# Half of a feed-forward chunk moved into the last attention step of a one-core transformer layer

## The reference

```
qkv = x @ w_qkv.T + b_qkv                      # x: (2, 1024, 512)
attn = softmax(q @ k.T / sqrt(32) + causal)    # per head, in float32
x = layernorm(x + (attn @ v) @ w_out.T + b_out)
hidden = relu((x @ sign(up_weight).T) * up_scale)
out = (hidden @ sign(down_weight).T) * down_scale * output_scale
return layernorm(x + out)
```

## Time and profile before

| | us |
|---|---|
| median of 3 runs | 776.65 (772.4 to 778.32) |
| the profiled execution | 774.34 |
| its span, first to last instruction | 772.6 |
| PE busy | 722.7 (94%) |
| DVE busy | 450.5 (58%) |
| POOL busy | 354.4 (46%) |
| ACT busy | 317.2 (41%) |

### The profile page before, as it was taken

How to read it: one execution, slowest core, us unless ns; L and a number is a source line. 1 busy time by engine, 2 the same in 40 slices (tenths; PEclk the granted TensorE clock), 3 DMA queues, 4 the chain that set the end, 5 groups by cost and what they waited for, 6 DMA issues and landing times.

```text
span 772.6 us, 11683 instructions
## 1 busy us (share of the span) xinstructions
PE 722.7 (94%) x4032; PEld 505.2 (65%) x4032; DVE 450.5 (58%) x1086; ACT 317.2 (41%) x631; POOL 354.4 (46%) x487
## 2 busy tenths in 40 slices
PE   6899999999999999999979889999999999999993
PEld 4788665655656556565544544788778787878882
DVE  4176495785967859678567751633294339334515
ACT  5211365654655546555546565432232222122210
POOL 4461467394673946739423502632353235223333
PEclk9999999999999999999999999999999999999998
DMA  6976464435544355452677331313012001000101
GB/s 231 296 208 177 110 174 124 136 105 163 150 132 132 108 157 148 115 133 88 174 206 261 109 123 58 120 32 119 14 41 95 28 1 41 15 1 12 44 1 54
DMA packets 44619, 85.71 MB, mean 111 GB/s; under 512 B 4880, under 2 KB 13584, under 8 KB 44432
## 3 DMA queue, kind: packets, MB, share of 16 engines
q1 hardware_dynamic: 35536, 79.72, 34.2%
q10 hardware_dynamic: 9024, 5.24, 2.4%
HBM read 55.33 MB, written 29.36 MB: 110 GB/s over the span
## 4 chain that ended last, share of the span: by engine, by line
PE 71%; DVE 19%; issue 3%; DMA 3%; POOL 2%; ACT 2%; SPq 0%; ACTq 0%; POOLq 0%
PE ps_heads L1045 9%; PE ps_proj L1087 7%; DVE heads_sb L835 7%; PE ps_proj L947 7%; PE ps_score L1104 6%; PE ps_unit L1063 6%; PE ps_unit L1087 5%; PE ps_sum L1039 5%; DVE maxes L813 5%; PE ps_unit L983 4%; PE ps_heads L1104 3%; PE ps_unit L1015 3%; PE ps_sum L1104 3%; PE ps_score L1015 2%; PE ps_score L983 2%
## 5 line engine op out<-in xcount | busy, mean ns | idle before, releaser
L655 POOL TENSOR_TENSOR hid_low<-hid_raw,hid_high 128x512 fp32r<-128x512 f32 x64 | 85.1, 1330 | 175.0 <-DVE hid_high L886 171.9
L711 ACT ACTIVATE probs<-ps_unit 128x512 f32<-128x512 f32 (+3 forms) x216 | 101.9, 490 | 88.4 <-PE ps_unit L1015 85.0
L619 POOL TENSOR_SCALAR_AFFINE_SELECT probs<-probs 128x128 f32<-128x128 f32 x256 | 73.1, 298 | 113.0 <-ACT probs L711 108.9
L711 ACT ACTIVATE probs<-ps_score 128x512 f32<-128x512 f32 (+3 forms) x155 | 75.2, 498 | 77.0 <-PE ps_score L1015 75.6
L886 DVE CAST hid_high<-hid_raw 128x512 fp32r<-128x512 f32 x64 | 27.1, 424 | 125.4 <-ACT hid_raw L766 125.2
L809 DVE CUSTOM_DVE_ANT_0 ps_unit<-ps_unit,causal 128x512 f32<-128x512 f32 (+3 forms) x162 | 80.1, 511 | 32.5 <-PE ps_unit L983 31.5
L1045 PE MATMUL ps_heads<-probs,v_rows 128*32 128x512 f32 (+3 forms) x768 | 80.3, 502 | 11.8 <-DVE heads_sb L837 11.8
L983 PE MATMUL ps_unit<-stack 96*128 96x512 f32 (+3 forms) x246 | 83.8, 354 | 5.7 <-DVE maxes L809 2.5
L1015 PE MATMUL ps_unit<-stack 98*128 98x512 f32 (+2 forms) x216 | 78.4, 366 | 4.1 <-DVE maxes L809 4.0
L613 POOL TENSOR_TENSOR parts<-qk_full,parts 128x512 fp32r<-128x512 f32 x32 | 41.3, 1289 | 64.7 <-ACT parts L690 64.4
L835 DVE RECIPROCAL heads_sb<-ps_sum 128x128 f32<-128x128 f32 x64 | 60.8, 950 | 9.2 <-PE ps_sum L1039 9.2
(11 more groups left out here) (195 smaller groups left out, 1478.0 us busy)
## 6 DMA issues: line engine op xcount, KB each, us to landing
stack<-qk_parts SPq DMA_DIRECT2D x96, 256.0 KB, 4.6
qk_parts<-parts SPq DMA_DIRECT2D x32, 512.0 KB, 2.9
v_all<-h_even ACTq DMA_DIRECT2D x16, 256.0 KB, 3.8
v_rows<-v_all SPq DMA_DIRECT2D x8, 512.0 KB, 4.3
heads_t<-heads_sb SPq DMA_DIRECT2D x16, 256.0 KB, 3.4
raw<-up_w SPq DMA_DIRECT2D x8, 512.0 KB, 3.9
x_tile<-x_rows SPq DMA_DIRECT2D x16, 256.0 KB, 5.5
raw<-down_w SPq DMA_DIRECT2D x8, 512.0 KB, 3.4
```

The costliest lines, as they stand in the source:

```text
L655: nc.gpsimd.tensor_tensor(hid[1][:, (HM * s + n) % 3, :], hid_raw[:, n % 2, :], hid[0][:, (HM * s + n) % 3, :].bitcast(FP32), ALU.subtract ...
L711: nc.scalar.activation(probs[:, (NP * s + n) % RING, 0:width], bank(what, s, n)[:, off:off + width], ACT.Exp, scale=SCALE).then_inc(s_exp, 1)
```

## The change

The first chunk's feed-forward is cut into two rounds of two tiles. Round 0 (tiles 0 and 1, matmuls of 256 columns in `up`, half as many in `down`) is placed in step 7 from slot 16 on, one pair each 1.95 slots, with hidden buffers of its own; it adds into two of the `ps_unit` banks. Round 1 (tiles 2 and 3) has the place of the old first chunk and 16 slots. With it:

- Scores of step 7 from piece 17 on rotate over two banks, and over three before that.
- In step 6, norm of the first half goes from slot 18.4 to 19.25, pv groups 4 to 6 go to 28, 30 and 32.2, and the last projection (k = 3) goes from slot 11.9 to 19.4; its keep goes from 19.9 to 29.4 and its stack from 22.2 to 31.9.
- Fetch 0 goes from slot 30 to 27.2, fetch_x 0 from 31 to 28.5. Jobs 0 and 1 go from 17.2 to 28, their signs from 23 and 25.5 to 31 and 33.5. All other jobs follow each 3.6 slots, with up and down weights in turn, and end in step 7.
- The output projection of tiles 0 and 1 goes into the end of step 6, that of tiles 2 and 3 early into step 7; layer norm and turns come some 13 slots earlier, over three banks.
- The last norm of step 7 goes to slots 55 to 58.6, inside round 1. The next chunk's split, projection and turns are packed over the 16 slots of round 1.

```
-ALONE = [[11.2, 13.5, 15.7, 18.3, 24, 28, 31.5, 36, 39.5, 43, 46.5, 50.3],
-ALONE_NORM = [[18.4, 18.41, 18.42, 18.43, 50.4, 50.41, 50.42, 50.43],
-              [17.6, 17.61, 17.62, 17.63, 48.7, 48.71, 48.72, 48.73]]
+ALONE_NORM = [[19.25, 19.26, 19.27, 19.28, 50.4, 50.41, 50.42, 50.43],
+              [17.6, 17.61, 17.62, 17.63, 55, 56.2, 57.4, 58.6]]
...
-LAST_BLOCK = [(1, 2, 4.2, 0.48, 9.9, 12.5, 14.9), (1, 3, 11.9, 0.45, 17.1, 19.9, 22.2)]
+LAST_BLOCK = [(1, 2, 4.2, 0.48, 9.9, 12.5, 14.9), (1, 3, 19.4, 0.62, 26.7, 29.4, 31.9)]
...
+ROUNDS = [(0, (0, 1)), (0, (2, 3))] + [(i, tuple(range(TT))) for i in range(1, CH)]
+TILES = [0, 2, 4, 8, 12, 16]
+FILL_FROM = 17
+
+JOBS = [("out", 0), ("out", 1), ("up", 0), ("up", 1), ("down", 0), ("up", 2), ("down", 1), ("up", 3), ("down", 2), ("up", 4),
+        ("down", 3), ("up", 5), ("down", 4), ("up", 6), ("down", 5), ("up", 7), ("down", 6), ("down", 7)]
...
-    signs = [late + 23, late + 25.5] + [late + 29 + 4.6 * k for k in range(4)] + [late + 50.2 + 4.5 * k for k in range(4)]
-    signs += [late + 88, late + 92] + [FIRST_UP + 1, FIRST_UP + 3] + [FIRST_UP + 7 + 2 * k for k in range(4)]
+    last = NP * (STEPS - 1)
+    signs = [late + 31, late + 33.5] + [late + 37 + 3.6 * k for k in range(16)]
-        put(late + 17.2 if k < 2 else signs[k - 2] + (3 if k < 4 else 0.5), "job", 0, k)
+        put(late + 28 if k < 2 else signs[k - 2] + 0.5, "job", 0, k)
...
-    last = NP * (STEPS - 1)
-    put(late + 30, "fetch", 0)
-    put(late + 31, "fetch_x", 0)
+    put(late + 27.2, "fetch", 0)
+    put(late + 28.5, "fetch_x", 0)
     put(last + 12, "fetch", 1)
+    for i in range(TT):
+        put(late + 36 + 1.7 * i, "split", 0, i)
+        put(late + 40 + 1.3 * i, "bias", 0, i)
         for m in range(12):
-            put(last + 0.5 + 5.2 * i + 0.42 * m, "attn", 0, 12 * i + m)
-        put(last + 5.8 + 5.2 * i, "y", 0, i)
-        put(last + 23 + i, "norm1", 0, i)
-        put(last + 26 + 2.5 * i, "turn", 0, i)
-    put(last + 22.5, "std1", 0)
+            put((late + 44.5, late + 47.1, last + 2.5, last + 5.5)[i] + 0.22 * m, "attn", 0, 12 * i + m)
+        put((late + 47, last + 2.2, last + 7.7, last + 8.2)[i], "y", 0, i)
+        put(last + 9.4 + 0.1 * i, "norm1", 0, i)
+        put((last + 12.9, last + 13.4, last + 15.2, last + 15.7)[i], "turn", 0, i)
+    put(last + 9.3, "std1", 0)
+    for r, (i, tiles) in enumerate(ROUNDS):
+        t = FIRST_UP + 16 * (r - 1)
         for m in range(HM):
-            put(t + m, "up", i, m)
-            if i < CH - 1 or m < HM - 2:
-                put(t + m + 2.5, "down", i, m)
-        if i == CH - 1:
-            for q in range(TT):
+            put(t + m if r else last + 16 + 1.95 * m, "up", r, m)
+            if r < len(ROUNDS) - 1 or m < HM - 2:
+                put(t + m + 2.5 if r else last + 20 + 1.95 * m, "down", r, m)
+        end = t + 17.55 if r else FIRST_UP + 1.2
+        for q in tiles:
+            put(end, "z", i, q)
+        if r and i + 1 < CH:
...
+                at = 2 * q if i else 2.7 * q
+                put(t + (2.2 + 0.7 * q if i else 0.3 * q - 0.8), "split", i + 1, q)
+                put(t + (3 + q if i else 1 + q), "bias", i + 1, q)
                 for m in range(12):
-                    put(t + 5.2 + 2 * q, "attn", i + 1, 12 * q + m)
-                put(t + 6 + 2 * q, "y", i + 1, q)
-                put(t + 6.7 + 2 * q, "ln1", i + 1, q)
-                put(t + 7.4 + 2 * q, "turn", i + 1, q)
+                    put(t + (5.2 if i else 3) + at, "attn", i + 1, 12 * q + m)
+                put(t + (6 if i else 4.2) + at, "y", i + 1, q)
+                put(t + (6.7 if i else 5.1) + at, "ln1", i + 1, q)
+                put(t + (7.4 if i else 6.4) + at, "turn", i + 1, q)
...
-            may = (2, 3, 4, 5) if s == STEPS - 1 else (0, 1, 2, 3, 4)
+            may = (2, 3, 4)[n >= FILL_FROM:] if s == STEPS - 1 else (0, 1, 2, 3, 4)
...
+        def attn_bank(s, i):
+
+            return ps_unit[0] if s else (ps_proj, ps_proj, ps_unit[0], ps_unit[1])[i]
+
+        def turn_bank(s, i):
+
+            return ps_unit[1] if s else (ps_proj, ps_unit[0], ps_unit[1], ps_unit[0])[i]
+
+        def down_bank(r, i):
+
+            return ps_unit[i] if r == 0 else ps_down[i - 2] if r == 1 else ps_down[i]
...
+                        act.wait_ge(s_score, NP * (STEPS - 1))
+                    if s == 1 and n == 0:
                         act.wait_ge(s_score, NP * STEPS)
...
-
                             pe.wait_ge(s_sign, 2)
                             pe.wait_ge(s_wol, 2)
-                    if s == 0 and m == 0 and i < 2:
-
-                        bank_read(last_user[i])
-                    if m == 0:
-
-                        wait(pe, s_y, TT * s + i - (s == 0))
-                    mm = nc.tensor.matmul(ps_attn[s > 0][i % 2][:, :], turned[s % 2][xp][:, c, i * P:(i + 1) * P], wo[wp][:, c, :],
+
+                            pe.wait_ge(s_qk, NB * STEPS)
+                        if s == 1:
+
+                            pe.wait_ge(s_z, 1)
+                    if s == 0 and m == 0 and i > 1:
+
+                        bank_read(last_user[i - 2])
+                    if m == 0 and (s > 0 or i == 1):
+
+                        wait(pe, s_y, TT * s + i)
+                    mm = nc.tensor.matmul(attn_bank(s, i)[:, :], turned[s % 2][xp][:, c, i * P:(i + 1) * P], wo[wp][:, c, :],
                                           start=(m == 0), stop=(m == 11))
...
-                    wait(pe, s_tl, TT * s + n)
+                    if s > 0 or n == 3:
+
+                        pe.wait_ge(s_tl, TT * s + n if s else 2)
+                    if s == 1 and n == 0:
+
+                        pe.wait_ge(s_z, 2)
...
+                    i, tiles = ROUNDS[s]
                     if n == 0:
-
-                        pe.wait_ge(s_tl, TT * (s + 1))
-                    if s == 0 and n < 2:
-
-                        bank_read(last_user[(5, 2)[n]])
+                        pe.wait_ge(s_tl, TILES[s + 1])
+                    if s == 0 and n == 1:
+
+                        bank_read(last_user[2])
                     if s == 0:
-                        pe.wait_ge(s_sign, 3 + n // 2)
+                        pe.wait_ge(s_sign, JOBS.index(("up", n // 2)) + 1)
 
                     wait(pe, s_hr, HM * s + n - 1)
                     for m in range(2 * DC):
-                        mm = nc.tensor.matmul(ps_up[n % 2][:, :], up_sb[n // 8][:, n % 8, m % DC, :],
-                                              turned[s % 2][m // DC][:, m % DC, :],
+                        mm = nc.tensor.matmul(ps_up[n % 2][:, 0:tokens(s)], up_sb[n // 8][:, n % 8, m % DC, :],
+                                              turned[i % 2][m // DC][:, m % DC, columns(s)],
                                               start=(m == 0), stop=(m == 2 * DC - 1))
...
+                    i, tiles = ROUNDS[s]
                     if s == 0:
-                        pe.wait_ge(s_sign, 11 + n // 2)
+                        pe.wait_ge(s_sign, JOBS.index(("down", n // 2)) + 1)
                     pe.wait_ge(s_hdl, HM * s + n + 1)
-                    if s == 0 and n == 0:
-                        pe.wait_ge(s_exp, NP * STEPS)
-                    for i in range(TT):
-                        if s == 0 and n == 0 and i == 2:
+                    for q in tiles:
+                        if n == 0 and s == 0:
+
+                            pe.wait_ge(s_tl, 4)
+                        if n == 0 and s == 1:
+
+                            pe.wait_ge(s_exp, NP * STEPS)
+                        if n == 0 and s == 2:
+
+                            pe.wait_ge(s_z, min(3 + q, 4))
                             pe.wait_ge(s_norm, QT * STEPS)
-                        if n == 0:
-
-                            wait(pe, s_z, TT * (s - 1) + i + 1)
+                        if n == 0 and s > 2:
+
+                            pe.wait_ge(s_z, TT * (i - 1) + q + 1)
                         for part in range(2):
-                            mm = nc.tensor.matmul(ps_down[i][:, :], hid[part][:, (HM * s + n) % 3, i * P:(i + 1) * P],
-                                                  down_sb[:, down_at(n), :], start=(n == 0 and part == 0),
+                            at = (q - tiles[0]) * P
+                            mm = nc.tensor.matmul(down_bank(s, q)[:, :], hidden(s)[0][part][:, (HM * s + n) % 3, at:at + P],
+                                                  down_sb[:, n, :], start=(n == 0 and part == 0),
                                                   stop=(n == HM - 1 and part == 1))
...
```

More of the change, by code:

```diff
@@ L387, in build @@
         up_b = sb(late, "up_b", [P, HM // 2, DC, P], FP32R)
+        hid0 = [sb(late, f"hid0_{n}", [P, 3, 2 * P], FP32R) for n in ("high", "low")]
+        hid0_raw = sb(late, "hid0_raw", [P, 2, 2 * P], FP32)
         t_odd = [sb(late, f"t_odd_{n}", [P, DC, HALF], FP32R) for n in ("high", "low")]
@@ L740, in _ @@
                         act.wait_ge(s_hl, 16 * (s + 1))
```

(16 more changed lines are left out.)

95 lines of the change are left out of this document (46 added, 49 removed).

## The result

The changed kernel takes 782.15 us (median of 10 runs, 779.23 to 785.01), the kernel before 775.56 us on the same chip (10 runs). The ratio is 1.0091, with a 95% interval of 1.0072 to 1.0110: 0.9% slower. The profiled execution takes 782.27 us against 774.34.

The account below looks back on a forecast made before the run. PE's waits in steps 6 and 7 were taken as what can be won. On the profiled 774.3 us the terms A to E, -4.8 - 1 - 3.3 + 1 + 15.2 = +7.1, gave 781.4, said as 781; range 764 to 790.

Parts of the forecast that it names:

- E: Step 6's moved transfers: keep lands behind 3.5 MB, stack after it, PE waits at unit 32; 15.2 us cost (9 to 21).
- A: Step 6, the norm: PE's 3.96 us gap and slow clock behind it go, some 1 us stays; 4.8 us gain.
- B: Border of steps 6 and 7: tile 0's output projection fills waits for the last maxima; 1 us gain (0 to 2).
- C: Step 7: up and down matmuls fill PE's waits, from 6.6 us to 3.3; 3.3 us gain (0 to 7).
- D: Feed-forward up: 256 matmuls of 256 columns replace 128 of 512; 1.0 us cost (0 to 2).
- R1: Step 6 transfers land before PE reaches unit 32: 766.2 us; chance 0.27 whole or in its larger part.
- R2: Filled step 7 runs at ACT's pace, each of 16 pairs costing 0.5 us: 789.4 us; chance 0.18.
- R3: Gaps at the border and in step 7 don't fill, B and C give nothing: 785.7 us; chance 0.15.

Follow-up runs that it names:

- e1: Changed kernel with the last projection, its keep and its stack back in their old slots (11.9, 19.9, 22.2): 774.95 us.
- e2: Changed kernel with only step 6's transfer order altered, keep (27) and stack (29) ahead of fetch 0 and fetch_x 0: 777.17 us.
- e5: Kernel before with only keep and stack of the last projection late (31.5, 34), behind fetch 0 and fetch_x 0: 791.97 us, ratio 1.0209.
- e11: e10 with the signs of jobs 0 and 1 at slots 27.5 and 30 in place of 23 and 25.5: 769.28 us, ratio 0.9913.
- e4: Changed kernel with all of step 6 as in the kernel before, step 7 and the feed-forward as changed: 775.05 us.
- e3: Changed kernel with only fetch_x 0 (1 MB) moved from slot 28.5 to 32, behind keep and stack: 779.98 us.
- e6: e1 with chunk 0's layer norm spread out (`std1` and `norm1` 2.2 slots later; projections, turns and ups moved too): 773.75 us.
- e8: Changed kernel with e7's transfer order and e6's spread layer norm, the moved projection kept: 771.71 us, ratio 0.9941; repeated on another chip, 772.23 us.
- e7: Changed kernel with step 6's keep at 27, stack at 27.9, around fetch 0, and fetch_x 0 (33) and the signs later: 775.56 us.
- e10: e8 with jobs 0 and 1 back at slot 17.2 and their signs at 23 and 25.5: 773.92 us.

## Why the prediction was right

781 was forecast and 782.15 measured. The mechanism is the one forecast, as e1, e2 and e5 show. That the number came within 1 us is in part luck: E was put 3 us too high, and the gains beside it 2.5 us too high as well. The sum can be tested term by term, by the profiled executions: +7.9 us in all. 1.2 us of these lie ahead of S1, in a part that the change doesn't touch.

**E, the transfers' order: right in its mechanism, 3 us too large.** Its dates came out as follows (forecast, then measured): fetch issued 402.5, 401.88; keep issued 406.6, 405.60; keep landed 417.8, 414.5; PE at unit 32 412.5, 411.7; its wait 11.5, 11.07; the wait for sign 0 1.9, 0.84. The slow clock and the refill after it cost 2.4 us (0.4, 0.83 and 0.98 beyond the full-rate distances of the next groups, and 0.2). Waits and slow clock together are 14.3 us.

Two steps of E were off, against each other. The pace: keep landed 3.3 us early, since these 12.6 us were forecast as 15.3. The prediction counted 3.5 MB (3.67 million bytes) in the 15.3 us of the kernel before, with the rest of one job ahead of fetch 0; two jobs of 512 KB (issued at 409.26 and 410.23, landed 4.2 and 4.5 us later) were still coming in, and the profile has 4.65 million bytes moved there, 304 GB/s. In the changed kernel it is 4.03 million and 320 GB/s. So the queue was hardly faster; the bytes were undercounted. The stack: PE could go on 8.2 us after the first stack DMA went out, where the prediction had 6.2 us (417.8 to 424). With PE 0.8 us early, these errors left the wait nearly that forecast.

What E is worth net is the difference of S1 and S2 between the changed kernel and e11, each without its attn matmuls: 64.1 - 51.9 = 12.2 us, against 15.2. The waits read by themselves say the same: 14.3 us, less the 1.52 and 0.69 us that e11 still waits for its stack and behind its first sign, is 12.1. The two ratios are 13.8 us apart, with some 3 us of uncertainty, and 2.4 of these belong to the layer norm that e11 also moved. Of E e1 shows 8.9, by moving the projection and its transfers alone; e5 shows 15.5 (791.97 against 776.49) in the kernel before.

**A and B, the norm's gap and the border: 5.0 in place of 5.8.** With the transfers out of the way, e11 has S1 and S2 without attn 5.0 us under those of before (56.86 - 51.9). A alone is 43.69 - 39.04 = 4.65 us, with 1.52 us of waiting still in it: the forecast was 4.8 with 1 us left. In the changed kernel itself the gap of 3.96 us went almost whole. B brought nothing: S2 less its attn matmuls is 13.17 us before, 12.8 in e11, 13.3 in e4 and 13.6 in the changed kernel, all within what one execution can tell. The wait of tile 1 for `y` of tile 0 (1.16 us), which the prediction named, eats the gain; the row maxima still make PE wait 0.52 us in e11.

**C and D, step 7: 0.6 us of gain in place of 2.3.** S3 and the rest behind it together are 4.6 us shorter, but 4.0 of these are the 17 attn matmuls that moved out. In e1 and e4 the same reckoning gives 0.3 and 0.5 us, in e3 1.9. This is the term that the prediction had most wrong for its size; the step that failed in it is the wait behind the table loads. Two matmul groups of four are 0.48 us apart, 0.12 each, as D had it. C's waits were others than forecast in size: 3.16 us behind the table loads where the forecast was 1.5, 1.2 us at down 1 for POOL's low part (1.1 forecast), none over 1 us in the filled stretch after that, and 1.2 us at chunk 1's second attn, which was not named. The table loads themselves took 1.28 us each, as before. What was undervalued is what stands ahead of them: `std1` also waits for `y` of the last tile.

The timeline of ACT in the changed kernel, with that wait:

```profile
456.69 1.28 ACT L781 ACT_TABLE_LOAD   x1 [1.80 <-DVE mom L890]
...
458.30 1.28 ACT L745 ACT_TABLE_LOAD   x1
459.59 0.55 ACT L745 ACTIVATE probs<-ps_score 128x256 f32<-128x256 f32 x2
```

1.80 + 2.90 us go from the end of ACT's work before to its next exponential: a score that needs one of two banks waits that long, less what it had in hand. Moving `std1` by 2.2 slots (e6) took the 3.16 us away; in e8 and e11, which have it, C and D gain 3.1 and 3.0 us by the same reckoning.

Sum by what was measured: -5.0 + 12.2 - 0.6 + 1.2 = +7.8, the difference of the spans. It has to add up, being made of differences of stretches; what tests it are the waits above.

**The rivals.** R1 (transfers in time, 766.2) didn't happen. e2 and e7, which put the transfers in time, gave 777.2 and 775.6, because each order that helps the stack delays signs or brings POOL's subtractions beside DVE's. e11, with both solved, has 766.36 in its profiled execution, but that match is chance: it has `std1` moved as well, worth 2.4 us that R1 didn't count, and its median is 769.28. R2 (ACT's pace) is refuted: behind the 3.16 us at the table loads the list of PE's waits has not one for an exponential up to chunk 1. R3 (nothing fills) is refuted by e11 for A, holds for B, and for about half of C (0.6 us and D's 1.0 are 1.6, of 3.3) as long as `std1` stands where the change put it.

Two things stay open. How much of the 5.6 us between e8's and e10's S2 is the contention of DVE and POOL, and how much the signs and the clock, was not taken apart. And what the 1.2 us ahead of S1 are: that part is the same in all kernels here, yet S1 starts at 375.26 (e3) to 377.34 us (e7), so they are within the spread of single executions.

## What to carry to other kernels

Moving a producer later moves its DMAs behind everything that is issued in between: add up the bytes that stand ahead, by what the profile says was moved and not by the list of issues, follow the second hop too (keep, then stack), and only then look at the engine's gap that the move was to fill. When a wait is gone and its time is not, compare the durations of single instructions with those of the version before: an instruction that lasts four times as long shows in no list of waits. And an activation that waits for a late weight holds the exponentials behind it, so its slot must be set by the landing of the transfer, not by the place where it is wanted.
